# Two batches through one correlation, peak search and weight spectrum in a three-stage block

## The reference, cut to what matters

```python
def _L1_attn_ref(x, Wq, bq, Wk, bk, Wv, bv, Wo, bo):   # x: (2, 1024, 256)
    H, Dk = 8, 32
    Q, K, V = proj(Wq, bq), proj(Wk, bk), proj(Wv, bv)  # (B, H, L, Dk)
    qf = jnp.fft.rfft(Q, axis=2)
    kf = jnp.fft.rfft(K, axis=2)
    corr = jnp.fft.irfft(qf * jnp.conj(kf), n=L, axis=2)
    corr_mean = corr.mean(axis=-1)                      # (B, H, L)
    w, delays = jax.lax.top_k(corr_mean, 13)            # 13 = int(2 * log(1024))
    w = softmax(w)
    ctx = sum over the 13 delays of w * (V rolled by the delay)
    return ctx @ Wo.T + bo

def _L1_ffn_ref(x, Wg, bg, W1, b1, W2, b2):
    topk_vals, topk_idx = jax.lax.top_k(x @ Wg + bg, 2)
    gates = softmax(topk_vals)
    return sum over the two chosen e of gate * (gelu(x @ W1[e] + b1[e]) @ W2[e] + b2[e])
```

## Time and profile before

| what | value |
|---|---|
| time, median of 3 runs | 445.28 us (443.12 to 446.82) |
| profiled execution, its own time | 444.77 us |
| its span | 443.0 us |
| mean granted clock of TensorE, share of full | 0.902 |
| busy in the span | PE 353.1, DVE 309.6, ACT 206.1, POOL 193.9 us |

### The profile page before, as it was taken

The page is one execution under the profiler, slowest core; times in us unless marked ns, Lnnn a source line. Parts: engine busy times, 40 slices in busy tenths (PEclk is TensorE's granted clock), DMA queues, the critical chain, the costliest instruction groups (busy, mean ns, idle before and its releaser), DMA issues.

```text
span 443.0 us, 8112 instructions
## 1 busy us (share of the span) xinstructions
PE 353.1 (80%) x2845; PEld 251.5 (57%) x2845; DVE 309.6 (70%) x713; ACT 206.1 (47%) x417; POOL 193.9 (44%) x148
## 2 busy tenths in 40 slices
PE   0989999999999998989796579324998888798233
PEld 0845766676666654555246435313888778788222
DVE  3456565556473599659998967595798878698275
ACT  1244666375653552315143345512776656475133
POOL 2203263324323141055366565106377777775322
PEclk9899999999999999969897689755999999899856
DMA  8910000000000530000227042502133333322395
GB/s 233 386 60 1 1 0 2 1 0 1 1 1 2 144 96 0 3 0 1 71 74 232 7 140 73 174 15 74 47 98 101 96 96 103 98 86 81 115 323 195
DMA packets 27272, 35.83 MB, mean 81 GB/s; under 512 B 7584, under 2 KB 22816, under 8 KB 27104
## 3 DMA queue, kind: packets, MB, share of 16 engines
q1 hardware_dynamic: 21152, 22.98, 16.0%
q0 software_dynamic: 3904, 10.24, 8.0%
q10 hardware_dynamic: 2176, 2.10, 1.4%
HBM read 26.00 MB, written 9.31 MB: 80 GB/s over the span
## 4 chain that ended last, share of the span: by engine, by line
PE 34%; DVE 24%; POOL 16%; issue 12%; DMA 7%; ACT 5%; SPq 1%; ACTq 0%; DVEq 0%; POOLq 0%
PE ps L1434 19%; POOL expert_rows_dram L546 6%; POOL late L542 6%; PE ps L1536 5%; PE ps L1668 3%; DMA late<-token_rows_dram,idx 3%; DVE t L1281 2%; DMA cols<-in_L_conv_bp_dram 2%; PE ps L1682 2%; POOL tiles L481 2%; PE ps L1646 2%; DVE sm L926 2%; DMA l<-expert_rows_dram 1%; DVE work L1016 1%; DVE tiles L1211 1%
## 5 line engine op out<-in xcount | busy, mean ns | idle before, releaser
L481 POOL TENSOR_TENSOR tiles<-tiles 128x1024 f16<-128x1024 f32 x16 | 34.6, 2164 | 79.0 <-ACT tiles L701 79.0
L542 POOL DMA_INDIRECT late<-token_rows_dram,idx x39 | 40.9, 1049 | 32.0 <-DVE idx L1217 20.4
L546 POOL DMA_INDIRECT expert_rows_dram<-late,idx x39 | 40.0, 1027 | 23.1 <-DVE late L1271 14.6
L788 ACT ACTIVATE late<-ps,b_sb 128x128 f32<-128x128 f32 x117 | 34.6, 366 | 32.7 <-PE ps L1668 29.5
L1434 PE MATMUL ps<-l 128*128 128x512 f16 x192 | 44.1, 379 | 2.1 <-ACT tiles L695 1.7
L1536 PE MATMUL ps<-u_h,tiles 128*128 128x256 f16 x256 | 44.6, 273 | 1.3 <-POOL tiles L481 1.3
L1668 PE MATMUL ps<-late,fwd_hi_sb 128*128 128x128 f16 x360 | 43.4, 230 | 0.0
L1668 PE MATMUL ps<-late,fwd_lo_sb 128*128 128x128 f16 x342 | 41.3, 223 | 0.3 <-DVE fwd_lo_sb L1257 0.3
L1682 PE MATMUL ps<-inv_hi_sb,late 128*128 128x256 f16 x180 | 40.2, 278 | 0.9 <-DVE late L1248 0.6
L1682 PE MATMUL ps<-inv_lo_sb,late 128*128 128x256 f16 x171 | 37.8, 272 | 0.8 <-DVE late L1271 0.7
L695 ACT ACTIVATE tiles<-ps,sm 128x1024 f32<-128x1024 f32 x16 | 17.8, 1114 | 43.7 <-DVE sm L928 43.7
(11 more groups left out here) (310 smaller groups left out, 876.1 us busy)
## 6 DMA issues: line engine op xcount, KB each, us to landing
prep<-in_L_ffn_W_dram SPq DMA_DIRECT2D x16, 384.0 KB, 3.3
l<-expert_rows_dram SPq DMA_DIRECT2D x16, 256.0 KB, 6.0
l<-in_x_dram SPq DMA_DIRECT2D x4, 512.0 KB, 7.6
token_rows_dram<-val SPq DMA_DIRECT2D x2, 1024.0 KB, 4.4
l<-in_inv_f_dram SPq DMA_DIRECT2D x1, 1536.0 KB, 6.8
out_dram<-l SPq DMA_DIRECT2D x3, 512.0 KB, 2.7
qk<-in_L_ffn_b_dram SPq DMA_DIRECT2D x8, 128.0 KB, 3.9
fwd_hi_sb<-in_fwd_hi_dram SPq DMA_DIRECT2D x1, 768.0 KB, 11.0
```

The costliest lines, as they stand in the source:

```text
L481: PL.tensor_tensor(Pt[1][:, n % 2, :], prob[:, n % 2, :], Pt[0][:, n % 2, :], ALU.subtract).then_inc(p_low, 1)
L542: pool.indirect_dma_start(gx[:, i % 6, :], None, xrows, bass.IndirectOffsetOnAxis(idx[:, 0, i:i + 1], 0)).then_inc(gathered[i % 6], 16)
L546: pool.indirect_dma_start(yrows, bass.IndirectOffsetOnAxis(idx[:, 1, s:s + 1], 0), ysb[:, s % 4, :], None).then_inc(scattered[s % 4], 16)
L788: last = ACTV(hf[:, s % 3, m * P:(m + 1) * P], psh[s % 2][:, m * P:(m + 1) * P], ACT.Gelu, bias=b1_sb[:, bass.ds(e, 1), m])
```

## The change

Six edits are made together.

1. `correlate`, `delays`, `weight_spectrum` and `w_fold` run once, on 16 rows (8 heads of both batches) where they ran twice on 8. The matrices `spec`, `wT`, `by_sum` and `wh_raw` are twice as wide. Each batch gets its own split Y and context, while their 32-bit scratch stays shared.
2. The order on every engine follows. PE: Q1 (eight), V1 (four), correlation, V1 (four), weight spectrum, inverse 0, inverse 1, output projection 0, gate 0, output projection 1, gate 1. ACT takes the exponential behind all copies of batch 1 and four expert casts, and the row writes of batch 0 move ahead of the casts 12 to 15. POOL does eight expert casts ahead of the first `weigh_imaginary`. DVE does both `apply_delays`, then both inverses, then the addition of batch 0. SP keeps its order.
3. `keep_awake` adds 38 products of 512 columns to PE, whose results nobody reads: 8 ahead of `rank`, 20 behind it and 10 behind `perm`.
4. The largest one-hot matrix is made by 32 operations of 128 columns with one scalar per row, where it was made by four of 1,024 columns with two tensors.
5. ACT applies one Gelu to a single element ahead of the tiles.
6. In the tiles, DVE's copy of the first weights goes ahead of the low part of the gathered rows.

```diff
-        for args in [("Q0", 2 * NT, "A"), ("D1_0", 2, "V", 1), ("D1_1", 2, "V", 1), ("C0", 2, "V"), ("Q1", 2 * SPLIT, "A"),
...
+        for args in [("Q0", 1, "A"), ("V0", 1, "A")] * NT + [
+                ("D1_0", 2, "V", 1), ("D1_1", 2, "V", 1), ("Q1", NT, "A"), ("V1", NT // 2, "A"), ("C", 2, "V"), ("V1", NT // 2, "A"),
+                ("wgm", 1, "V"), ("T", 1, "V"), ("W", 1, "V"), ("I0", 4, "V"), ("I1", 4, "V"), ("O0", 8, "V"), ("YT0", 4, "A"), ("gate0", 2, "V"),
...
             cross_products(0)
+            cross_products(1)
+            for n in range(8):
+                expert_low(n)
             weigh_imaginary(0)
-            cross_products(1)
-            for n in range(2):
-                expert_low(n)
+            weigh_imaginary(1)
             context_low(0)
...
-            delays(0)
-            take_qkv(1, range(5))
-            y_hi(0)
-            take_qkv(1, range(5, NT))
-            for n in range(2):
+            for k in range(NT):
+                take_products("Q1", k)
+            for k in range(NT):
+                take_products("V1", k)
+            for n in range(4):
                 expert_high(n)
...
+            delays()
             for n in range(4, 8):
                 expert_high(n)
...
+            act.wait_ge(gexp_ready, 1)
+            ACTV(hf[0:1, 0, 0:1], gt[0:1, 1, 0:1], ACT.Gelu)
...
-                for q in range(0, 2 * TT, 8):
-                    V.tensor_tensor(onehot_p[:, q:q + 8, :], iota128.unsqueeze(1).to_broadcast([P, 8, P]),
-                                    slot[:, 1, q:q + 8].unsqueeze(2).to_broadcast([P, 8, P]), ALU.is_equal).then_inc(perm_part, 1)
+                for q in range(2 * TT):
+                    last = V.tensor_scalar(onehot_p[:, q, :], iota128, slot[:, 1, q:q + 1], None, ALU.is_equal)
+                    if q % 8 == 7:
+                        last.then_inc(perm_part, 1)
...
-            w_fold(0)
+            w_fold()
             apply_delays(0)
-            cross_spectrum(1)
+            apply_delays(1)
             inverse(0)
-            delays(1)
-            add_attention(0)
-            w_fold(1)
-            for j in range(0, 6):
-                V.bn_stats(tst[:, j, :], t1[:, 0, j, :])
-            apply_delays(1)
+            inverse(1)
+            add_attention(0, stats=True)
+            token_stats(0, NT - 1)
             gate_take(0)
...
             for i in range(TILES + RESULT_LAG):
                 if i < TILES:
+                    copy_first(i)
                     gathered_low(i)
-                    copy_first(i)
...
-                    last = PE.matmul(dst[0:HEADS, :], sp_(k), odd(inv32, k), start=(k == 0), stop=(k == 3))
...
+                    last = PE.matmul(dst[0:ROWS, :], sp_(k), odd(inv32, k), start=(k == 0), stop=(k == 3))
...
+            for j in range(NT):
+                project(1, j, "Q")
+            for j in range(NT // 2):
+                project(1, j, "V")
+            correlate()
+            for j in range(NT // 2, NT):
+                project(1, j, "V")
...
-            weight_spectrum(0)
-            project(1, range(SPLIT, NT))
+            weight_spectrum()
             inverse(0)
-            correlate(1)
+            inverse(1)
             out_project(0)
...
+            def keep_awake(n):
+
+                for _ in range(n):
+                    PE.matmul(bank(fills("YT1")[-1]), ident16, const16[:, 0:4 * P], start=True, stop=True)
```

More of the change, by code:

```diff
@@ L622, in xf_hi_part, with take_products, delays @@
                 ACTV(xf[0][:, part, :], xf32[b][:, part, :], ACT.Identity).then_inc(xf_high, 1)
[L624 to L635 removed]
+            def take_products(name, k):
+                f = fills(name)[k]
+                if name == "Q1" and k == 0:
+                    act.wait_ge(spec_ready, 1)
+                if name[0] == "Q":
+                    take(f, qk[:, k, :], bank(f)[:, 0:512])
+                else:
+                    take(f, val[int(name[1])][:, k, :], bank(f)[:, 0:256])
+            def delays():
+                act.wait_ge(peak_ready, 1)
+                ACTV(dspace[2][0:ROWS, :], dspace[0][0:ROWS, :], ACT.Exp, bias=top[:, 16:17], scale=1.0 / (N * DK)).then_inc(exp_ready, 1)
             def y_hi(b):
@@ L735, in _ @@
             take_tokens(1)
-            take_qkv(0, range(6))
+            for k in range(6):
+                take_products("Q0", k)
+                take_products("V0", k)
             xf_hi_part(1, 0)
             xf_hi_part(1, 1)
-            take_qkv(0, range(6, NT))
+            for k in range(6, NT):
+                take_products("Q0", k)
+                take_products("V0", k)
             out_bias_high()
@@ L1355, in _ @@
             xf_low(1, 1)
-            cross_spectrum(0)
-            for m in range(CC):
-                for k in range(2):
-                    x_low(1, m, k)
-            delays(0)
+            cross_spectrum(0, (0,))
+            for k in range(2):
+                x_low(1, 0, k)
+            cross_spectrum(0, (1,))
+            for k in range(2):
+                x_low(1, 1, k)
             out_bias_low()
+            cross_spectrum(1)
+            delays()
             f = FIRST["wgm"]
@@ L1555, in spectra_even, with project @@
                 last.then_inc(filled, 1)
-            def project(b, chunks=range(NT)):
+            def project(b, j, part):
                 pe.wait_ge(late_in, 16 * 5)
                 wait_taken(pe, fills(f"D{b}_1")[1])
-                for j in chunks:
-                    for lo, n in ((0, 512), (512, 256)):
-                        more = [(dc_row[:, :], qkv_row[:, lo:lo + n])] if j == 6 else []
-                        product(fill(f"Q{b}")[:, 0:n], [(hl(xhat, S, k, slice(j * P, (j + 1) * P)), hl(qkvW, S, k, slice(lo, lo + n))) for k in range(CC)],
-                                more).then_inc(filled, 1)
@@ L1568, in correlate @@
-            def correlate(b):
+                lo, n = (0, 512) if part == "Q" else (512, 256)
+                more = [(dc_row[:, :], qkv_row[:, lo:lo + n])] if j == 6 else []
+                product(fill(f"{part}{b}")[:, 0:n], [(hl(xhat, S, k, slice(j * P, (j + 1) * P)), hl(qkvW, S, k, slice(lo, lo + n))) for k in range(CC)],
+                        more).then_inc(filled, 1)
+            def correlate():
                 pe.wait_ge(inv32_in, 16)
-                pe.wait_ge(spec_ready, b + 1)
+                pe.wait_ge(spec_ready, B)
@@ L1752, in _ @@
             gate(0, 1)
-            inverse(1)
             out_project(1, range(4))
```

163 lines of the change are left out of this document (77 added, 86 removed).

## The result

The changed kernel took 456.58 us (median of 4 runs), beside 444.41 us for the kernel before. One of the four (466.46) fell into a slower state of the chip and is left out of the ratio, which is 1.0222, 95% interval 1.0163 to 1.028. A second set of runs on another chip gave 1.0246 (1.0217 to 1.0274). So it is slower by 2.2 to 2.5%. The forecast was slower, with 451 as the likeliest time in a range of 444 to 458. The sign was right and so, in the main, was the place; the loss was nearly twice as large as the sum had it. The profiled execution took 455.58 us.

What follows compares the result with a forecast made beforehand. Bound by a serial chain of waits across engines, then by POOL's gathers and scatters over 39 tiles. Routing +8.8, one-hot −1.0, tiles −2.3 sum to +5.5 on 444.77, 450.3, given as 451; range 444 to 458.

Steps and rivals of the forecast that it cites:

- a, b): Batch 1's Q starts at 176.4; Q, bias and copies end at 188.5, the cross spectrum's second half adds 6.6: 195.1.
- c): Shared correlation on PE costs the same as one, 6.6 us with its first half slow after PE's idle, ending at 201.7.
- d to f): From correlation's end at 201.7, through V's last four, expert casts, exponential and weights, to POOL's first product at 226.7.
- h): DVE's part of an inverse takes 7.0 us; two follow one another, ending at 262.7.
- i): Addition 0 with statistics 5.3, last transposes and copy, then gate 0 at 3.99; projection 1 starts at 273.1, 7.9 later.
- j): Projection 1's first three products slow, +1.9; batch 0's row writes no longer ahead of batch 1's tokens, −1.0; routing 8.8 late.
- k): Large one-hot as 32 operations takes 3.5 instead of 4.55, −1.0 us; at the 32-bit rate 6.4, so +1.9.
- l): Start of the tiles: earlier Gelu table load, PE kept running and earlier weight copy gain 2.3 us; dummy products cost nothing.
- (e): On ACT the exponential waits behind V copies and four experts' high casts, in rounds of 5.8; DVE waits 7.5 us.
- Step f: DVE's weights are ready at 223.2, POOL's eight low casts end at 226.7, so POOL ends last, by 3.5 us.
- slow one-hot: Rival, chance 0.2: one-hot at one element a cycle and no gain at the tiles, 456 us, 458 at most.
- Hidden casts: Rival, chance 0.15: expert weights load fast enough that POOL paces rounds at 3.3; POOL starts 5.9 earlier, total 445.

Runs made afterwards that it cites:

- casts between: Changed kernel with ACT's exponential ahead of all expert casts and POOL's low casts four before, two between, two behind the contexts' products: 455.36 us, ratio 1.0202.
- casts late: Changed kernel with the exponential ahead of all expert casts, four POOL casts before the contexts and casts 4 to 11 moved to the inverses: 449.1 us, ratio 1.0048.

## Why the prediction came out as it did

The path was in the main the forecast one. The part that costs most, casts queued ahead of a single chain, was shown by the two runs that moved them: with the casts between it moved and the total did not, with the casts late the total followed. That gate 0 ahead of projection 1 costs time was shown on its stretch alone; no run turned it into a gain. The sizes were too small. By the prediction's steps, against both profiles of the changed kernel:

| step | forecast | first profile | second profile |
|---|---|---|---|
| a) start of Q | 176.4 | 178.1 | 176.3 |
| a, b) Q to correlation | 18.7 | 19.2 | 19.5 |
| c) correlation | 6.6 | 7.0 | 7.0 |
| d to f) its end to POOL's first product | 25.0 | 26.0 | 26.1 |
| g) contexts | 10.5 and 11.5 | 10.5 and 11.5 | 10.5 and 11.5 |
| h) both inverses on DVE | 14.0 | 14.4 | 15.8 |
| i) addition 0 to projection 1 | 10.4 | 10.9 | 8.8 |
| j) projection 1 to rank, against before | +0.9 | +1.2 | +3.2 |
| rank, against before | +8.8 | +13.7 | +13.6 |
| k) one-hot | −1.0 | +0.7 | +0.7 |
| l) first gather to first scatter | −2.3 | −2.0 | −2.0 |

- At rank 4.9 and 4.8 were missed, but at different steps. Q started at 176.0 to 176.5 in six of the eleven profiles with the shared correlation, and at 178.1 to 178.9 in five. Yet the late start does not explain the first profile: the second started on time and lost its lead in steps h and j. In h, the low part of context 1 (L1147) took 3.97 beside a subtraction and a cast of POOL instead of 2.52 (casts late, with no cast beside it: 1.91); in j, all of projection 1 was slow (7.51 and 6.53 for its halves, against 7.61 and 4.46).
- Two prices were left out of the sum, or put at nothing. One is PE's lower clock behind a wait or behind small products. I charged it for the correlation (c) and for three products of projection 1 (j). It also met the first products of Q and the weight spectrum (3.59 instead of 1.95) in both profiles, gate 0 in the first (5.62 for 3.99) and all of projection 1 in the second. The other is DVE beside a cast of POOL, which I feared only for the peak search; it met the weights in f and the low part in h.
- Of the 13.7 late against before, 2.3 lie in the base: that profile was early at rank (286.01, against 288.26 and 288.39 in two profiles of kernels that are the same up to there). Counted from those it is some 11.4, near the loss of the totals. The forecast of rank itself, 286.0 + 8.8 = 294.8 for 299.7, misses by 4.9 whatever the base.
- The chain through the casts (e) was right in every link: rounds of 5.8 (208.07, 213.88, 219.75, 225.47) and a wait of 8.2 for 7.5.
- Step f's "POOL ends last, by 3.5" was wrong: DVE's weights ended last, by 0.25. The weight spectrum was slower, and one small DVE operation took 1.59 beside the last cast instead of 0.19.
- Step k had the wrong rate. 0.163 for 128 columns lies between the two bounds (0.11 and 0.2), nearer to the 32-bit row.
- Step l was right on its total, but not on all its parts. The table load and the copy bring 1.7 of the 2.0. "With PE kept running the first two tiles go at 1.34 instead of 1.99" did not come for the first tile, whose 18 products took 1.93 behind the dummies. The dummy products did not lie on the chain ahead of rank: PE waited 2.18 behind them. Another 1.3 was won between the first and the last scatter (95.65 for 96.98; 0.7 in the second profile), which no step held.
- That 456.58 lies within 444 to 458 is luck in part. It lies outside the forecast's 448.5 to 453.5, and the upper end was set by the slow one-hot, with 1.9 lost there and nothing gained at the tiles; 0.7 was lost and 2.0 gained. The time came near that end for other reasons, those above.
- "Hidden casts" was the rival with the wrong lever. It asked for faster loads. The lever was where the casts run: POOL's two-tensor subtraction and DVE's two-tensor operations hold one another up, so casts queued beside the contexts cost the chain about as much as casts queued ahead of them.

## What to carry to other kernels

Before merging two independent chains into one, ask what each did while the other waited: here the eight low casts that stood between the two batches' products on POOL had the second batch's work as their cover, and once merged, they stood in line. Filler on POOL was free here beside DVE operations that read PSUM; place it there, and not "somewhere in the idle time". A wait on a serial chain is paid twice when PE comes out of it at the lower clock, so charge the product behind every new wait at the lower rate. And take a second profile before explaining a difference of 2 us link by link: here two executions of one program lost their time at different links.

## What the hardware showed beyond what I expected

- DVE and POOL hold one another up in operations with two SBUF tensors, and the price is large: 2.54 instead of 1.23 for 1,024 columns on DVE, 5.19 instead of 3.23 for two casts on POOL. The Trainium skill states this as a rule: by "SBUF — State Buffer", section "Who interferes with whom", a DVE instruction with two SBUF inputs contends with a GpSimd instruction that reads SBUF, and the port pair that they share is an exclusive lock. The traces agree: 2.5 beside the cast, 1.2 without, and an operation with one PSUM input keeps its 0.69.
- One SBUF tensor is not always safe. In the casts between, DVE's own cast of 128 columns ran as long as POOL's beside it, 1.69 (rows below), and takes 0.23 in the changed kernel, without one. `by_sum`, 16 columns of one tensor, took 1.29 there instead of 0.22. The maximum over 1,024 columns kept its 1.22 beside POOL's casts (208.34 in the changed kernel).
- PE's clock fell under work, too. In the changed kernel it was still 1.00 in 272 to 273 us, at the start of gate 0, 0.51 in the next microsecond, and 0.50 until 286 with PE busy throughout; ahead of that PE had idled 0.7 in 270 to 272. The same 32 products kept 1.00 as gate 1 (292 to 296). So small products alone do not settle it.
- Behind 45 dummy products that ran up to it the weight spectrum took 1.95; behind 14 that ended 5.5 us ahead of it, 3.59, as with none.

The rows of the second point, from the timelines of POOL and DVE of the casts between:

```profile
216.27 1.64 POOL L488 TENSOR_TENSOR l<-prep,l 128x768 f16<-128x768 f32 x1 [0.16 <-ACT l L668]
...
216.30 1.69 DVE L1083 CAST wT_h<-l 128x128 f16<-128x128 f32 x1
```
